# Half of the edge attributes' walk inside the message pass, and the stage behind it cut to 52 slots

## The reference, cut to what matters

```python
# layer 0: messages over the edges, summed by destination, then an update and a norm
msg_in = jnp.concatenate([x[row], x[col]], axis=-1)
messages = jax.nn.relu(msg_in @ W_msg + b_msg)
aggregated = jax.ops.segment_sum(messages, col, num_segments=x.shape[0])
h = jax.nn.relu(jnp.concatenate([x, aggregated], axis=-1) @ W_upd + b_upd)
# ... layer norm of h with gamma and beta
# layer 1: edge attributes (96 values per edge), sum, count and maximum by destination
out1 = jax.ops.segment_sum(edge_attr, col, num_segments=n)
out2 = jax.ops.segment_max(edge_attr, col, num_segments=n)
out3 = out1 / jnp.maximum(cnt, 1.0)
h = jnp.concatenate([x, out1, out2, out3, u[batch]], axis=1)
h = jax.nn.relu(h @ W1 + b1) @ W2 + b2
```

## Time and profile before

| what | value |
|---|---|
| median of 3 runs | 2459.43 us (2450.95 to 2461.61) |
| the profiled execution's own time | 2459.7 us |
| its span, first to last instruction | 2457.9 us |
| mean granted PE clock, share of full | 0.713 |
| DVE busy | 1449.4 us (59%), 3645 instructions |
| POOL busy | 1414.0 us (58%), 1447 instructions |
| PE busy | 1134.3 us (46%), 5278 instructions |
| ACT busy | 455.6 us (19%), 952 instructions |
| DMA | 433.85 MB, mean 177 GB/s |

### The profile page before, as it was taken

The page is one execution under the profiler, slowest core; times in us unless marked ns, Lnnn a source line. Parts: engine busy times, 40 slices in busy tenths (PEclk is TensorE's granted clock), DMA queues, the critical chain, the costliest instruction groups (busy, mean ns, idle before and its releaser), DMA issues. The chain is left out here.

```text
span 2457.9 us, 20304 instructions
## 1 busy us (share of the span) xinstructions
PE 1134.3 (46%) x5278; PEld 805.4 (33%) x5278; DVE 1449.4 (59%) x3645; ACT 455.6 (19%) x952; POOL 1414.0 (58%) x1447
## 2 busy tenths in 40 slices
PE   7788888887576279999900000000024111111105
PEld 5577777675243145655600000000023000000004
DVE  6699998887878532232146677776664334434432
ACT  3122222221011111112200000000014333333332
POOL 3677777774235210000167777777743777777774
PEclk9899999999666579999955555555557555555557
DMA  6777877775656410000046666666634666666664
GB/s 181 233 248 239 253 238 245 237 240 179 233 181 216 154 39 10 10 9 9 18 151 210 211 210 206 205 206 208 210 118 132 209 213 208 208 213 211 207 208 143
DMA packets 200168, 433.85 MB, mean 177 GB/s; under 512 B 40757, under 2 KB 116422, under 8 KB 200052
## 3 DMA queue, kind: packets, MB, share of 16 engines
q1 hardware_dynamic: 130888, 249.67, 28.5%
q0 software_dynamic: 67936, 182.02, 27.4%
q10 hardware_dynamic: 1228, 0.87, 0.1%
HBM read 262.80 MB, written 169.57 MB: 176 GB/s over the span
## 5 line engine op out<-in xcount | busy, mean ns | idle before, releaser
L393 POOL DMA_INDIRECT msg_rows<-message_source_table,source x416 | 399.0, 959 | 169.6 <-issue 122.2
L1818 POOL DMA_INDIRECT att_rows<-att_table,lane_source x416 | 419.3, 1008 | 126.7 <-issue 126.7
L1839 POOL DMA_INDIRECT att_rows<-message_source_table,lane_source x416 | 393.5, 946 | 156.6 <-issue 126.4
L1922 PE MATMUL late_ps<-ident,att_largest 128*4 128x128 f32 x1 | 0.4, 376 | 549.9 <-DVE att_largest L2048 549.9
L516 PE MATMUL msg_ps_sum<-msg_by_edge,msg_rows 128*128 128x128 f32 x1664 | 210.1, 279 | 58.0 <-DVE aggT L649 58.0
L1970 PE MATMUL late_ps<-w_selfT,hT 128*125 128x256 f32 x100 | 49.8, 649 | 400.1 <-DVE x L2207 400.1
L516 PEld LDWEIGHTS msg_ps_sum<-msg_by_edge,msg_rows 128*128 128x128 f32 x1664 | 194.0, 192 | 95.5 <-issue 95.2
L1394 POOL DMA_INDIRECT att_terms<-aggT,first_edge x25 | 29.5, 1180 | 323.8 <-ACT aggT L1518 323.8
L504 PE MATMUL msg_ps_window<-msg_window,msg_by_node 128*128 128x256 f32 x832 | 207.5, 393 | 12.0 <-DMA msg_window<-message_window_table 12.0
L2200 DVE SCALAR_TENSOR_TENSOR att_rows<-att_rows,lane_line,late_ps_share 128x256 f32<-128x256 f32 x208 | 99.9, 480 | 167.1 <-ACT late_ps_share L1902 158.0
L2070 DVE SCALAR_TENSOR_TENSOR aggT<-aggT,lane_carry,att_rows 128x260 f32<-128x260 f32 x388 | 190.3, 490 | 13.6
(11 more groups left out here) (326 smaller groups left out, 2361.9 us busy)
## 6 DMA issues: line engine op xcount, KB each, us to landing
att_states<-aggT SPq DMA_DIRECT2D x104, 528.0 KB
msg_window<-message_window_table SPq DMA_DIRECT2D x416, 128.0 KB
best_states<-att_rows SPq DMA_DIRECT2D x104, 512.0 KB
attr_states<-aggT SPq DMA_DIRECT2D x32, 768.0 KB
attr_states<-attr_work SPq DMA_DIRECT2D x20, 768.0 KB
attr_work<-in_edge_attr SPq DMA_DIRECT2D x23, 384.0 KB
msg_rows<-message_source_table,source POOLq DMA_INDIRECT x416
att_rows<-att_table,lane_source POOLq DMA_INDIRECT x416
```

The costliest lines, as they stand in the source:

```text
L393: nc.gpsimd.indirect_dma_start(rows[:, s, t, :], None, self.source_table, bass.IndirectOffsetOnAxis(ap=self.source[:, at:at + 1], axis=0)) ...
L1818: nc.gpsimd.indirect_dma_start(rows[:, t % ring, :], None, self.attention_table, bass.IndirectOffsetOnAxis(ap=self.lane_source[:, t:t + 1] ...
L1839: nc.gpsimd.indirect_dma_start(best_rows[:, g % SLOTS, t, :], None, self.source_table, bass.IndirectOffsetOnAxis(ap=self.lane_source[:, g ...
```

## The change

Twice as many tiles of the walk are done in the message pass: `walk` is called twice per slot, as share 0 where it was and as share 1 between the third `accumulate` and `by_nodes`. That makes 208 tiles in 26 steps; SP stores a step every four slots. The stage behind keeps 208 tiles, so its loop has 52 slots. The fifths of the update are seven slots apart and no longer 13 (`UPD_SLOTS` stays 26). The search waits for its levels at slots 28 and 46 (the hand-over of the second moves to slot 32). PE's order is written by slots, with `multiply` at d = -4 to 0, `base` at 8, 9 and 11 to 13, and `turn` at 21 to 23.

```diff
-UPD_PERIOD = 13
-UPD_SLOTS = 2 * UPD_PERIOD
-WALKED = LANE // TG // STEP_TILES
+UPD_PERIOD = 7
+UPD_SLOTS = 26
+WALK_TILES = 2
+WALKED = LANE // TG * WALK_TILES // STEP_TILES
...
                     def fetch_window(i, s):
-                        if i > 0 and s == STEP_TILES - 2 and i * SLOTS + s >= STEP_TILES + 6:
-                            store_walk(i - 1)
+                        done = i * SLOTS + s - 6
+                        if done > 0 and done % (STEP_TILES // WALK_TILES) == 0:
+                            store_walk(done * WALK_TILES // STEP_TILES - 1)
...
                     pipelined(sp, [(fetch_window, 0)])
+                    store_walk(WALKED - 2)
                     store_walk(WALKED - 1)
...
-                    def walk(i, s):
+                    def walk(i, s, share):
-                        t = i * SLOTS + s
-                        if s == 0:
-                            dve.wait_ge(*self.past(walk_in[i % 2], 16 * (i // 2 + 1)))
-                            if i >= 2:
-                                dve.wait_ge(*self.past(walk_out[i % 2], 16 * (i // 2)))
+                        t = (i * SLOTS + s) * WALK_TILES + share
+                        k, at = t // STEP_TILES, t % STEP_TILES
+                        if at == 0:
+                            dve.wait_ge(*self.past(walk_in[k % 2], 16 * (k // 2 + 1)))
+                            if k >= 2:
+                                dve.wait_ge(*self.past(walk_out[k % 2], 16 * (k // 2)))
...
-                    pipelined(dve, [(acc[0], 0), (add, 3), (acc[1], 0), (hot[0], 4), (walk, 0), (hot[1], 4),
-                                    (acc[2], 0), (by_nodes, 5), (acc[3], 0)])
+                    walked = [of_tile(walk, share) for share in range(WALK_TILES)]
+                    pipelined(dve, [(acc[0], 0), (add, 3), (acc[1], 0), (hot[0], 4), (walked[0], 0), (hot[1], 4),
+                                    (acc[2], 0), (walked[1], 0), (by_nodes, 5), (acc[3], 0)])
...
-                    for c in range(len(parts) + 1):
-                        if c < len(parts):
-                            for b in parts[c]:
-                                multiply(b)
-                            for b in parts[c][0:2]:
-                                base(b)
-                        if c == 0:
+                    def update_work(c, d):
+                        b0 = parts[c].start
+                        if d == 21:
+                            turn(b0)
+                            turn(b0 + 1)
+                        if d == 22:
+                            turn(b0 + 2)
+                        if d == 23:
+                            turn(b0 + 3)
+                            turn(b0 + 4)
+                        if 8 <= d < 10:
+                            base(b0 + d - 8)
+                        if 11 <= d < 14:
+                            base(b0 + d - 9)
+                        if -4 <= d < PART - 4:
+                            multiply(b0 + d + 4)
+                    for s in range(-4, UPD_PERIOD * (len(parts) - 1) + UPD_SLOTS):
+                        for c in range(len(parts)):
+                            if -4 <= s - UPD_PERIOD * c < UPD_SLOTS - 2:
+                                update_work(c, s - UPD_PERIOD * c)
+                        if s == 6:
                             spread_heads()
-                        if c == len(parts):
-                            shift()
-                        if c > 0:
-                            for b in parts[c - 1]:
-                                turn(b)
-                        if c < len(parts):
-                            for b in parts[c][2:PART]:
-                                base(b)
+                    shift()
...
-                        if s == 40:
+                        if s == 28:
                             dve.wait_ge(level_in[0], 16 * NB)
...
-                        if s == 44:
+                        if s == 32:
                             known()
                             nc.vector.tensor_copy(at[1][:], place).then_inc(located, 1)
-                        if s == 70:
+                        if s == 46:
                             dve.wait_ge(level_in[1], 16 * NB)
```

More of the change, by code:

```diff
@@ L650, in accumulate @@
                                                 ).then_inc(tile_added[t], 1)
-                    def walk(i, s):
-                        t = i * SLOTS + s
-                        if s == 0:
-                            dve.wait_ge(*self.past(walk_in[i % 2], 16 * (i // 2 + 1)))
-                            if i >= 2:
-                                dve.wait_ge(*self.past(walk_out[i % 2], 16 * (i // 2)))
-                        row = walk_rows[:, i % 2, s * AF:(s + 1) * AF]
+                    def walk(i, s, share):
[5 more added lines that the diff above has]
+                                dve.wait_ge(*self.past(walk_out[k % 2], 16 * (k // 2)))
+                        row = walk_rows[:, k % 2, at * AF:(at + 1) * AF]
                         before = walk_held[:, (t - 1) // STEP_TILES % 2, (t - 1) % STEP_TILES, :]
@@ L663, in walk @@
                         nc.vector.scalar_tensor_tensor(
-                            out=walk_held[:, i % 2, s, 0:AF], in0=before[:, 0:AF] if t > 0 else self.lowest[:],
+                            out=walk_held[:, k % 2, at, 0:AF], in0=before[:, 0:AF] if t > 0 else self.lowest[:],
                             scalar=self.lane_line[:, t:t + 1], in1=row, op0=ALU.min, op1=ALU.max).then_inc(self.maxed, 1)
@@ L668, in walk @@
                         nc.vector.scalar_tensor_tensor(
-                            out=walk_held[:, i % 2, s, AF:2 * AF], in0=before[:, AF:2 * AF] if t > 0 else self.none[:, 0:AF],
+                            out=walk_held[:, k % 2, at, AF:2 * AF], in0=before[:, AF:2 * AF] if t > 0 else self.none[:, 0:AF],
                             scalar=self.carry[:, t:t + 1], in1=row, op0=ALU.mult, op1=ALU.add).then_inc(self.summed, 1)
@@ L1207, in search @@
                             nc.vector.tensor_copy(at[0][:], found).then_inc(located, 1)
-                        if s == 40:
+                        if s == 28:
                             dve.wait_ge(level_in[0], 16 * NB)
                             not_over(SLICES, levels[:], slice(0, NB), within)
-                        if s == 41:
+                        if s == 29:
                             count(within, inside)
-                        if s == 42:
+                        if s == 30:
                             known()
@@ L1216, in search @@
                                                                 in1=inside, op0=ALU.mult, op1=ALU.add))
-                        if s == 43:
+                        if s == 31:
                             known()
                             link(nc.vector.tensor_scalar(place, place, -1.0, None, ALU.add))
-                        if s == 44:
+                        if s == 32:
                             known()
                             nc.vector.tensor_copy(at[1][:], place).then_inc(located, 1)
-                        if s == 70:
+                        if s == 46:
                             dve.wait_ge(level_in[1], 16 * NB)
                             not_over(SLICES, levels[:], slice(0, NB), within)
-                        if s == 71:
+                        if s == 47:
                             count(within, inside)
-                        if s == 72:
+                        if s == 48:
                             known()
@@ L1232, in search @@
                             assert steps == found_all
-                        if s == 73:
+                        if s == 49:
                             known()
                             nc.vector.tensor_scalar(found, place, -1.0, None, ALU.add).then_inc(searched, 1)
-                        if s == 74:
+                        if s == 50:
                             dve.wait_ge(searched, found_all + 1)
```

## The result

The changed kernel takes 2403.78 us (median of 4 runs, 2402.19 to 2406.61) and the kernel before, run beside it, 2460.52 us; the ratio is 0.9785, 95% interval 0.9773 to 0.9797. The profiled execution has a span of 2400.3 us against 2457.9, so 57.6 less.

The account below looks back on a forecast made before the run. The message pass was taken as DVE's at first and POOL's at the end, both close; the stage behind as DVE's. Pass +36.3 and stage -61.4 us make -25.1: 2434.5 us, range 2419 to 2452.

Parts of the forecast that it names:

- the gap: Message pass: DVE's 13 unexplained gaps, 20.3 us, come once per trip and stay; taken as 0, at most +4 us.
- The message pass otherwise: Message pass: 104 more walk tiles cost DVE +47.6 us, and row waits of 11.3 us go: +36.3 us.
- The sign: Message pass: some 540 us from DVE's first `accumulate` to its last, 498 before, would show the forecast right.
- SP's queue at 0: Message pass: 13 more store waits and 15 MB more traffic on SP are covered by four window buffers: 0.
- The walk out of the stage, -47.6: Stage behind: 104 fewer walk tiles, 26 slots of eight instructions, save DVE 47.6 us.
- PE by slots, -29.5: Stage behind: products four slots ahead end the relu waits of 7 us; 4.0 of 33.5 us of waits stay: -29.5 us.
- a load on PE: Stage behind: fifths seven slots apart make PE as busy as DVE; falling clock costs +2 us, bounds 0 and 90.
- The second rival: Stage behind: PE drops to 1.2 GHz and paces it; 2463 us, or 2445 to 2455 if partial; chance 0.17.
- The search, +13.7: Stage behind: DVE waits 7.5 and 6.2 us for two batches of search gathers, +13.7 us, bounds 0 and 22.
- The end, 0: End of stage behind: last `turn` and `shift` end 3 us later, hidden by DVE's 5.2 us state wait: 0.
- The slower rival: Message pass: PE falls to 1.2 GHz, 2.8 us per slot, 2490 us with 20 slots; 0.09 together with late windows.
- The last rival: Message pass: POOL still paces, gaps overlap new work, pass grows 20 to 25 us: 2421 us; in a shared 0.14.

Follow-up runs that it names:

- e1: The changed kernel with share 1 of the walk moved straight behind share 0, ahead of the second one-hot: 2450.46 us, ratio to before 0.996.
- e4: The changed kernel with one walk tile per slot, so only the change to the stage behind: 2435.59 us, ratio to before 0.9893.
- e5: The kernel before with only PE's order written by slots; fifths 13 slots apart, search in its old slots: 2446.7 us, ratio 0.9958.
- e9: e5 with 11 matmuls of the identity in each of PE's seven idle slots per fifth: 2438.2 us, ratio to before 0.9928.
- e2: The kernel before with its one walk tile per slot moved behind the third accumulate: 2464.05 us, ratio 1.0014.
- e6: The changed kernel with share 1 of the walk behind the last accumulate of the slot: 2407.46 us, ratio to before 0.9801.
- e12: The kernel before with the walk's 384 KB load issued one window fetch behind its 768 KB store, not directly behind it: 2456.93 us, ratio 0.9998.
- e3: The kernel before with SP's store and load of the walk one window fetch later, DVE's program untouched: 2460.81 us, ratio 1.0002.
- e8: The changed kernel with six matmuls of the identity in PE's slot 10 of the stage behind: 2401.08 us, ratio to before 0.9775.

## Why the prediction was wrong

The spans of the two profiled executions differ by 57.6 us, so the error is 57.6 - 25.1 = 32.5 us. It is made of 36.3 - 15.4 = 20.9 in the message pass, 67.2 - 61.4 = 5.8 in the stage, 2.8 behind the loop and 3.0 in attention.

- *The step that failed* is the gap: "The gaps come once per trip; if they grow with the instructions of a slot (12 for 10), it is 20% of 20.3, +4 us; I take 0." It took 20.3 us of idle time as fixed because the trace seemed to name no cause, and gave it a bound on the dear side only. The cause was in the trace, as a register load of DVE that took 2709 ns and not 593, 0.8 us behind SP's store. The change moves the instruction on which that store hangs past the register load. e1 puts it back, and loses 46.7 us. In what it measured, the term is -20.0 and not 0.
- *The message pass otherwise*: 47.6 of walk and -11.3 of row waits were right; with -20.0 for the gaps they make 16.3 against a measured 15.4. The sign "some 540 us from DVE's first `accumulate` to its last" does not follow from the sum (498 + 36.3 is 534); measured are 514.9 us (96.9 to 611.8).
- *SP's queue at 0*: right as a cost (PE never waits for a window; the store waits, 194.0 us in 25 and so as long apiece as before, fell on a queue with lead), but it was looked at only for what it delays, not for what its transfers do to other engines' loads.
- *The walk out of the stage, -47.6*: from e4 to the changed kernel the stage falls from 213.8 to 164.8, 49.0 us, of which 3.7 are a shorter search wait (6.3 to 2.6). Right, within the 4 us by which the stage varies.
- *PE by slots, -29.5*: the sum is near, the cause is not. Relu waits went (-31.6) and `base` waits came (+4.9): -26.7. But the order alone is worth 10 us, or 5.6 in the stage's length (e5); 11 more by the medians, 12.6 in the stage's length, came with the nearer fifths, which the prediction had priced only as a load on PE (+2).
- *The second rival* was set aside with "a PE that falls behind has no pauses, and without pauses its matmuls went back to full speed". In the changed kernel it ran 26 us at half speed without a pause, and again from 725 us to the end of the stage. That cost little, since most products were early enough: the waits for PE's products are 4.9 us in all, where +2 was taken. With fifths 13 apart the clock cost some 8 us (e5 to e9).
- *The search, +13.7*: mis-sized. 2.6 us came, and 3.1 for the heads and 3.0 for `shift`, which were not forecast: 8.7. It had taken the long gathers of 4.3 us over; they were gone, though a bound of 0 was given for that. Its own terms give 12 x (1.83 + 1.2) + 1.83 = 38.2 us for DVE's way to the first wait, and not 39.7, so its sum was 1.5 us short.
- *The end, 0*: -2.8, the last wait of 5.2 us being 2.4.
- *The slower rival*, PE at 1.2 GHz in the message pass: clock 1.00. Did not happen.
- *The last rival*, gaps that overlap with the new work: the pass grew by even less than its 20 to 25 us, but not for that reason. With the same work and both shares early the gaps are 45.3 us (e1).

## What to carry to other kernels

Idle time that a trace puts down to no releaser still has a cause; before it is carried over as a constant, the engine's queue instructions (register loads among them) are to be read for one that is longer than its fellows, and what the other queues sent just before it. An instruction that another queue waits for sets when that queue's transfers go out, so its place within the slot can be worth more than its own duration. And when two engines are level, a gap removed on one (e2, e6) is paid back as waits for the other: the move paid because the work it brought used the time that the gaps set free.

## What the runs showed of the hardware that was not expected

- A load of eight window bases into DVE's registers takes 593 to 612 ns over the pass of the changed kernel (its first alone takes 846). In the kernel before it takes 1664 to 2727 ns at the twelve steps where it starts 0.8 us behind a store of 768 KB and, at all but the last, 0.4 us behind a load of 384 KB on SP's queue. Behind the store alone (e12) it takes 1420 to 2102 ns. Moving both by one window fetch (e3) or parting the two (e12) halves the sum of the gaps. What the load waits for inside the chip, no run shows.
- After one pause of 3.96 us PE stayed at 1.2 GHz for 26 us of unbroken matmuls; behind one of 1.96 us (e8) it was there for about 17, and from 680.7 to 684 us of the changed kernel with no pause ahead. In the kernel before it was back within some 10 us of the stage's start. What makes the difference is open.
- The search's gathers took up to 4.3 us apiece in the kernel before and in e5 and e9, up to 2.8 us in e4 and 2.3 and 2.6 us in the changed kernel's two profiles. What decides that was not tried by itself.
